# Joining the two halves of a quantised block with VectorE instead of a transfer, and loading behind the block's store

## What is computed

```python
x = x + tanh(g_xattn[0]) * L0_xattn(layernorm(x), ctx, ...)   # 32 query heads of 128, 8 key heads, 64 keys
x = x + tanh(g_ffn[0])   * L0_ffn(layernorm(x), ...)          # 4-bit weights
x = x + tanh(g_xattn[1]) * L1_xattn(...)
x = x + tanh(g_ffn[1])   * L1_ffn(...)                        # experts
x = x + tanh(g_xattn[2]) * L2_xattn(...)
x = x + tanh(g_ffn[2])   * L2_ffn(layernorm(x), w1, w2, w3)   # weights quantised, see below
x = x + tanh(g_xattn[3]) * L3_xattn(...)
x = x + tanh(g_ffn[3])   * L3_ffn(...)
```

```python
absmax = max(abs(flat), axis=1)
normalized = flat / where(absmax == 0, 1, absmax)
idx = searchsorted((CODE[:-1] + CODE[1:]) * 0.5, normalized)
w_dq = (CODE[idx] * absmax)
```

## Time and profile before

| | us |
|---|---|
| runs, median of 3 (lowest, highest) | 1565.34 (1561.07, 1567.39) |
| the profiled execution, its own time | 1562.88 |
| its span | 1561.1 |
| busy in the span: PE, DVE, ACT, POOL | 1377.6, 1110.0, 666.3, 353.5 |

### The profile page before, as it was taken

One profiled execution on the slowest core, in us unless ns is written; L12 is line 12 of the kernel. 1 busy time (PEld: TensorE's weight loads), 2 busy tenths in 40 slices (PEclk: granted clock), 3 DMA queues, 4 the chain that ended last, 5 costly groups with the idle time before them and its releaser, 6 DMA issues.

```text
span 1561.1 us, 18735 instructions
## 1 busy us (share of the span) xinstructions
PE 1377.6 (88%) x6532; PEld 988.7 (63%) x6532; DVE 1110.0 (71%) x2045; ACT 666.3 (43%) x1395; POOL 353.5 (23%) x395
## 2 busy tenths in 40 slices
PE   6999999989897979987999997999999999999204
PEld 5665566556475648664788875677777777777201
DVE  4688888887887997946455564666665666668998
ACT  3777777776523443422222223444444444343104
POOL 1112221222154020321311111122122122122530
PEclk9999999999998999976999998999999999999557
DMA  5699999999810011412321310011011011000001
GB/s 210 167 219 215 209 227 219 213 212 214 211 69 0 1 31 57 93 32 61 76 68 47 105 55 14 27 41 68 27 41 68 27 42 68 1 1 1 0 1 55
DMA packets 40136, 136.42 MB, mean 87 GB/s; under 512 B 5184, under 2 KB 11200, under 8 KB 33840
## 3 DMA queue, kind: packets, MB, share of 16 engines
q0 software_dynamic: 13824, 51.91, 17.9%
q1 hardware_dynamic: 26224, 83.38, 16.1%
HBM read 72.63 MB, written 10.75 MB: 53 GB/s over the span
## 4 chain that ended last, share of the span: by engine, by line
PE 57%; DVE 17%; DMA 16%; DVEq 3%; ACT 2%; issue 2%; POOL 1%; POOLq 0%; SPq 0%
DMA AR<-AR 15%; PE PS L150 12%; PE PS L152 11%; PE PS L151 11%; PE PS L899 4%; PE PS L935 4%; DVE AR L663 2%; DVE AR L2485 2%; PE PS L921 2%; DVE AR L2474 2%; DVE AR L2481 2%; PE PS L1458 1%; PE PS L264 1%; PE PS L529 1%; DVE X L2524 1%
## 5 line engine op out<-in xcount | busy, mean ns | idle before, releaser
L432 POOL DMA_DIRECT2D AR<-AR x92 | 91.0, 1006 | 349.9 <-DMA AR<-AR 144.2
L529 PE MATMUL PS<-R,PT 128*128 128x512 f32 x256 | 120.1, 613 | 13.0 <-DVE X L703 12.3
L151 PE MATMUL PS<-R16r 128*128 128x512 f32 (+1 forms) x328 | 122.8, 374 | 0.0
L152 PE MATMUL PS<-R16r 128*128 128x512 f32 (+1 forms) x312 | 119.6, 383 | 0.0
L504 PE MATMUL PS<-R,HT 128*128 128x256 f32 x512 | 115.9, 379 | 0.0
L601 ACT ACTIVATE s_sb<-PS,sm 128x64 f32<-128x64 f32 x256 | 76.2, 324 | 69.4 <-DVE sm L688 69.4
L504 PEld LDWEIGHTS PS<-R,HT 128*128 128x128 f32 x512 | 94.8, 190 | 11.6
L1044 ACT COPY AR<-PS 128x512 f32<-128x512 f32 x64 | 37.5, 586 | 144.7 <-PE PS L152 144.3
L529 PEld LDWEIGHTS PS<-R,PT 128*128 128x128 f32 x256 | 48.3, 194 | 71.5 <-issue 69.8
L150 PE MATMUL PS<-HTr,R16r 128*128 128x512 f32 (+1 forms) x240 | 89.9, 375 | 3.0 <-DVE R16r L188 1.6
L150 PE MATMUL PS<-R16r,HTr 128*128 128x512 f32 (+1 forms) x224 | 90.2, 403 | 0.0
(11 more groups left out here) (309 smaller groups left out, 3539.4 us busy)
## 6 DMA issues: line engine op xcount, KB each, us to landing
AR<-AR POOLq DMA_DIRECT2D x92, 528.0 KB, 5.7
OR<-in_wo SPq DMA_DIRECT2D x12, 1024.0 KB, 7.7
dequantised<-AR SPq DMA_DIRECT2D x8, 1056.0 KB, 5.4
WR<-in_w0q SPq DMA_DIRECT2D x8, 1024.0 KB, 8.7
AR<-in_w3q SPq DMA_DIRECT2D x8, 1024.0 KB, 4.9
WR<-dequantised SPq DMA_DIRECT2D x22, 256.0 KB, 2.8
AR<-in_nf SPq DMA_DIRECT2D x4, 1056.0 KB, 7.1
nf_in<-in_nf SPq DMA_DIRECT2D x4, 1056.0 KB, 6.9
```

The lines of the kernel that those rows point to most:

```text
L151: nc.tensor.matmul(out, ah, bl, start=False, stop=False)
L152: return nc.tensor.matmul(out, al, bh, start=False, stop=last_)
L432: nc.gpsimd.dma_start(nf_below(g)[:, part], what[:, part], accum_op=ALU.add, max_dma_last_dim=4 * N_NF // 2).then_inc(added, 16)
L529: i = nc.tensor.matmul(bank(5 + tt), PT[:, at:at + P], vo[:, pr, b, :], start=pr == 0, stop=pr == 1)
```

## The change

DVE does the join instead of a transfer, in unit b = 0 of the next turn (`joined`), for groups 0 to 6; the last group keeps `join`. Five additions a group are left in the transfers' count (`nf_added`), and NSUM is 10 with the new step. `up` with k = 0 loses its wait. The store waits for DVE's step. SP's order becomes: store of g - 1, then the loads of nf and o for g + 1 and kv and q for g + 2. `nf_max` of the next group moves from b = 0 to b = 1.

```diff
-        NSUM = NUP + 1
+        NSUM = NUP + 2
         def nf_added(g, k):
-            return 16 * (g * NDOWN + k)
+            return 16 * (g * (NDOWN - 1) + k)
         def nf_store(sp, g):
-            sp.wait_ge(A0["nf_left"], nf_added(g, NDOWN))
-            sp.wait_ge(A0["nf_right"], nf_added(g, NDOWN))
+            if g == LATE:
+                sp.wait_ge(A0["nf_left"], nf_added(g, NDOWN))
+                sp.wait_ge(A0["nf_right"], nf_added(g, NDOWN))
+            else:
+                sp.wait_ge(A0["nf_summed"], (g + 1) * NSUM)
...
             for g in range(NG):
                 if g:
+                    nf_store(sp, g - 1)
                     if g + 1 < NG:
                         load_nf(g + 1)
-                    nf_store(sp, g - 1)
+                        load_o(g + 1)
+                    if g + 2 < NG:
+                        load_kv(g + 2)
                 if g + 2 < NG:
                     load_q(g + 2)
-                    load_o(g + 2)
-                if g + 3 < NG:
-                    load_kv(g + 3)
...
         def join(pool, g):
-            pool.wait_ge(A0["nf_summed"], (g + 1) * NSUM)
+            pool.wait_ge(A0["nf_summed"], (g + 1) * NSUM - 1)
...
                 for k in range(1, NDOWN):
                     accumulate(pool, g, k)
-                join(pool, g)
...
             if g or m > 2:
-                act.wait_ge(A0["nf_summed"], g * NSUM + (m - 1 if m > 2 else m - 2))
+                act.wait_ge(A0["nf_summed"], g * NSUM + (m - 1 if m > 2 else m - 3))
...
             if k == 0:
-                if g:
-                    dve.wait_ge(A0["nf_left"], nf_added(g - 1, NDOWN))
-                    dve.wait_ge(A0["nf_right"], nf_added(g - 1, NDOWN))
                 nc.vector.tensor_scalar(nf_above, nf_in(g), bound, rise, ALU.is_gt, ALU.mult)\
...
+        def joined(dve, g):
+            dve.drain()
+            dve.wait_ge(A0["nf_left"], nf_added(g, NDOWN - 1))
+            dve.wait_ge(A0["nf_right"], nf_added(g, NDOWN - 1))
+            nc.vector.tensor_tensor(nf_below(g), nf_below(g), nf_above, ALU.add).then_inc(A0["nf_summed"], 1)
...
-                if more and b == 0:
+                if g and b == 0:
+                    joined(dve, g - 1)
+                up(dve, g, 2 * b)
+                if more and b == 1:
                     nf_max(dve, g + 1)
-                up(dve, g, 2 * b)
...
                 if b == 0:
+                    joined(dve, LATE - 1)
                     dve_f0_nibbles(dve)
```

## The result

| | before | changed |
|---|---|---|
| runs, median of 4 each (lowest, highest) | 1564.94 (1561.07, 1567.39) | 1590.87 (1590.59, 1592.17) |
| the profiled execution's span | 1561.1 | 1589.4 |
| ratio of times | | 1.017, 95% interval 1.0148 to 1.0191 |

The change costs 26 us, 1.7%. Fewer bytes are moved (GpSimd's queue 44.34 MB against 51.91), and the kernel is slower.

The account below looks back on a forecast made before the run. A serial chain of accumulating transfers was taken to bound the first stage. Turns 1 to 5 +27.4, turn 6 +3.6 and turn 7 +1.5 made +32.5 on 1562.88, 1595.4, stated as 1596 us; range 1572 to 1609.

Parts of the forecast that it names:

- Forecast and sign: Whole kernel: SP's burst of transfers delays addition pairs 1 to 3; 1596 us, slower with chance 0.83.
- VectorE's own sum: VectorE's steps in a first-stage turn, with the join and moved nf_max: 49.5 us without a DMA wait.
- The queues' term: Mask 5 starts at turn start T + 39.2: 14.5 us of SP transfers stand before or between pairs 1 to 3.
- From mask 5 to the next turn: VectorE's end of a turn: 18.27 us, in which the 2.02 us wait for ScalarE stays.
- Turn 6: Last turn with this work, without kv and q but with the next stage's first loads: 53.5 us, +3.6.
- Turn 7 and after: Turn 7 gets the last join on a full VectorE: 0 to 2.5 us, taken as 1.5.
- Covers: Delays hidden by the longer turn: PE stands some 5 us for o, ending at T + 56 at most, below 57.5.
- PE waiting on OR: Sign that the forecast is right: PE waits for the buffer OR, into which o is loaded.
- The range: Total time of 1572 to 1609 us, leaving out the faster and no-change cases.
- the turn's term: Length of each of turns 1 to 5 with SP's burst: 57.5 us, its ends 54.3 and 59.6.
- The faster rival: First-stage additions hide SP's loads, pairs keep near 5.62 us, every DMA wait goes: -16.3 us, 1547; chance 0.12.

Follow-up runs that it names:

- run 1: Changed kernel with SP's order of before (nf, store, q, then o and kv at the turn's end), join still by VectorE: 1557.22 us, ratio 0.9958.
- run 5: Kernel before with SP's new order and nf_max in unit 1, the join still a transfer: 1584.37 us, ratio 1.0116.
- run 4: Changed kernel with the load of o cut to a sixteenth of its columns from group 2 on: 1572.05 us, ratio 1.0049.
- run 7: run 1 with the load of q also held back behind addition 3: 1558.56 us, ratio 0.9952.

## Why the prediction was right, point by point

- *Forecast and sign.* 1596 forecast, 1590.9 measured, slower with the mechanism named. The mechanism is shown from both sides: SP's order put back gives 0.9958 (run 1), SP's order together with nf_max's place gives 1.0116 without the join (run 5), and 2.7 us less in the burst give 2.3 us less a turn (run 4). That the sum came within 5 us is in part luck: turns 1 to 5 were forecast 9.8 us too long, and turn 6, turn 7 and what lies behind brought 6.0 more than forecast, 3.2 of it by no mechanism of the prediction.
- *VectorE's own sum*: 49.5 a turn without DMA waits. Right: run 1 has 50.17 with 0.68 of wait. The join took 2.36 at T + 5.6, and nf_max never waited in unit 1.
- *The queues' term*, 14.5 us in front of pair 3 on top of three pairs, mask 5 at T + 39.2. Measured T + 36.5. The term was mis-sized: one burst costs 13.1 us of the engines, not 14.5, and three pairs 16.5, not 16.9; that is 1.8 of the 2.7. With them the sum gives T + 37.3, and 0.8 stay open. The wait came nearly all at mask 4, for pair 2 (4.98 us in turn 3, 0.20 at mask 5): mask 5 follows mask 4 by 5.2 us, of which 5.0 are DVE's own steps.
- *From mask 5 to the next turn*: 18.27 forecast, 18.99 measured, with a new wait of 0.89 for ACT's `far` in unit 3. Turn: 57.5 forecast, 55.5 measured, +17.6 for turns 1 to 5 instead of +27.4.
- *Turn 6*: +3.6 forecast, +5.4 measured. Mask 4 waited 8.71 there; the next stage's loads stand in the burst too.
- *Turn 7 and after*: +1.5 forecast. SP's load behind the first use of the 4-bit weights came 447.86 - 422.75 = 25.1 later, the turn's start 22.6: the whole 2.5 of the join. A further 3.2 us lie behind it, in stages whose code is the same. Executions with this code differ by more than that: from turn 7's start to the end the changed kernel's profiled execution takes 1589.4 - 432.00 = 1157.4 us, and run 1, with the same code there, 1553.5 - 400.42 = 1153.1; the other runs with VectorE's join lie between 1152.9 and 1157.2. What makes these executions differ is open; the mean granted clock of TensorE (0.928 here, 0.939 before and in run 1) does not order them, since run 7 has 0.938 with 1156.6.

```profile
447.86 0.33 SPq L1380 DMA_DIRECT2D WR<-in_l1wqv  x1
```

- *Covers.* PE's stand at o was small (2.8 us in all from 100 to 430), less than the 5 us a turn I gave it, and was hidden. The sign "PE waiting on OR" thus came out only faintly. DVE's waits at the masks went to 37.7, about 6 a turn; I said 8. The wait was at masks 4 and 5, as forecast, not at mask 3. SP issued store, nf, o and kv within 3.3 us, where I said 2, and the DMA share was 0.75, as I said.
- *The range.* Its lower end, 1572, is said to be a bound of the turn's term, but the shortest turn worked out (54.3) gives 1579. The measured time lies inside either.
- *The faster rival* would have needed additions and loads to be served side by side. It came out only where the loads were put elsewhere, at -7.3 us (run 1) against its -16: the loop from mask 2 to mask 5 was not in that rival's sum.

## What to carry to other kernels

A transfer saved is worth something only where the chain is waiting for the engines. Here VectorE's join and nf_max in unit 1 were worth -0.4% with the loads spread over the turn, and with the loads in a burst the join was worth nothing in a turn. When loads are moved "behind" an instruction, add up all that now starts at that one instant and ask which serial chain of transfers starts there too. A longer turn cannot be read off one engine's book of work and waits: in the changed kernel more than half of the loss stood there as VectorE's join, and without the join (run 5) it stood there as waits. And an early product needs an early place: mask 2, made sooner, only waited for the store of the block it overwrites.

## What the runs showed of the hardware

**The two queues were served in turn.** In turn 3 of the changed kernel the additions had the engines from 218 to 222 us (first two lines), and SP's burst had them from 226 to 230 us, with no packet of an addition among its own (third line). The profile sums the times of the packets, so a share can pass 100% a little.

```profile
q0 software_dynamic: 197, 0.76, 101.1%
q1 hardware_dynamic: 16, 0.05, 3.1%
...
q1 hardware_dynamic: 220, 1.65, 100.8%
```

From 217 to 237 us the shares were 65.2% and 36.4%, together the whole of the engines' time, and the additions moved 1.40 MB in these 20 us. Right after it, from 241 to 247 us, they were alone and moved 1.12 MB in 6 us.

```profile
q1 hardware_dynamic: 954, 4.73, 65.2%
q0 software_dynamic: 363, 1.40, 36.4%
...
q0 software_dynamic: 298, 1.12, 97.7%
```

**An addition held the engines longer than SP's transfers of the same size.** In the changed kernel, 150 to 360 us, 49.8% went to 20.01 MB of additions and 25.0% to 19.14 MB of SP's, 1.9 times as long for a byte.

**SP's transfers took less engine time in one burst than spread among the additions.** For the 4.78 MB of a turn it was 13.1 us in the changed kernel and 13.3 in run 5, both with the burst, against 14.8 in the kernel before and 14.1 in run 1 (26.8% for 19.15 MB, below), both with the old order. No run says why.

```profile
q1 hardware_dynamic: 3840, 19.15, 26.8%
```
